# Attention phase: three PSUM banks for the row maxima and one for the scores, in place of two and two

## The chip, the cores and the metric

One core of a Trainium2 chip runs the kernel. The metric is the device time of one execution in microseconds (us); the time before is the median of three runs.

## The reference, cut to what matters

`x` is 8 batches of 512 rows of 512 numbers, `ctx` the same size. Two layers follow each other; each adds a gated attention and a gated feed-forward to `x`. Only the first attention is touched by the change:

```
xn = layernorm(x)                       # over the last axis
q, k, v = xn @ W_Q + b_Q, ctx @ W_K + b_K, ctx @ W_V + b_V   # 16 heads of 32
scores = einsum('bhqd,bhkd->bhqk', q, k) / sqrt(32)
attn = softmax(scores, axis=-1)
out = einsum('bhqk,bhkd->bhqd', attn, v) # 512 numbers a row again
x = x + tanh(g_xattn[0]) * (out @ W_O + b_O)
x = x + tanh(g_ffn[0])   * ffn(layernorm(x))         # quantised weights and activations
x = x + tanh(g_xattn[1]) * attention(layernorm(x), ctx)
x = x + tanh(g_ffn[1])   * linear(mxfp4(layernorm(x)))
```

Everything is float32.

## The kernel before, in words

The program has four phases one after the other: `attention_phase` (the projections and the first attention up to the normalised heads), `prepare_weights`, `ffn_phase` and `final_phase`. A barrier and a clearing of the semaphores stand between the first and the rest. The change lies in `attention_phase` alone.

**Work of the attention phase.** The 8 batches each have G = 4 groups of J = 4 heads. A group has 16 steps i (4 heads times T = 4 tiles of 128 rows). For each step there is a *maxima* matmul (L406): queries as the weights, keys as the moving operand, 96 rows deep, because each float32 operand is kept as a high and a low part and three products are stacked. VectorE takes the negated maximum of each of its 128 rows (L565). When a group's 16 are done, `mt` (L412) transposes them, ScalarE copies them to a row (L501), and a DMA puts that row as row 97 under the stacked queries (L334). Then the *score* matmul (L423) computes the transposed scores with the maximum already subtracted, and ScalarE takes the exponential straight from PSUM into `probs` (L510). GpSimd adds up the probabilities of the four key tiles (L619, 12 adds a group). After 16 steps TensorE multiplies probabilities and values (`pv`, L434, 32 matmuls) and sums the rows (`den`, L444, 8 matmuls); VectorE takes reciprocals in four pieces (L571) and multiplies (L576), ScalarE adds a bias (L515).

**What lies between.** In the same stream TensorE makes the projections of later groups: queries and keys (L381, three matmuls a step, copied out by ScalarE as the high part, L480, and by VectorE as the low part, L557, then stored to HBM at L320 and loaded back stacked at L328), the values (L395, copied by ScalarE, L496), and the transposes of `x` and `ctx` (L365, high part by ScalarE, L471, low part by VectorE, L549). LayerNorm of `x` is done by VectorE (L536, L541), GpSimd and ScalarE (L488).

**The order** is written out by hand. `Clock` holds every step with a time; a group has a PERIOD of 160 units, of which the first 128 are 16 slots of 8 units, and the rest is for `pv` and `den`. Each engine emits its own instructions sorted by that time plus an offset of its own, for all batches, with no loop. So the order in each queue is fixed, and only semaphores decide when things start. In a slot TensorE has a maxima matmul of a later group (19 slots ahead of its scores), a score matmul, and what projection work falls there. ScalarE's copies L480 and L471 stand between the exponentials; `mt`'s copy L501 stands before the exponential of slot 14.

**PSUM** has eight banks of 128 x 512 float32: two `work` banks for projections and transposes (given out by `Turns`), two `mx` for the maxima, two `sc` for the scores, one `pvb`, one `den`. A wait before a matmul says that its bank has been read. For the maxima it is `mx_done` (one count per reduce, L565), for the scores `exp_done` (one per exponential, L510); both are for the count that leaves one later instruction open, since there are two banks:

```
wait_count(pe, mx_done, it, shift, G * T * J, g * T * J + i - 1)
wait_count(pe, exp_done, it, shift, G * T * J, g * T * J + i - 1)
```

The third number of `wait_count` is the count per batch, the last the count within it; it emits a wait on the product of both, and none if that isn't positive.

Of the kernel before, what the change touches and what calls it, by code (L numbers as in the profile page):

```python
# [5 lines left out]
ALU = mybir.AluOpType  # L6
ACT = mybir.ActivationFunctionType
AX = mybir.AxisListType

P = 128  # L10
# [124 lines left out]
def attention_phase(nc, NB, x, ctx_in, w_q, b_q, w_k, b_k, w_v, b_v, spill, attn_t, ctx_t):  # L135
# [4 lines left out]
    T, C, G, J = S // P, D // P, D // P, P // DH  # L140
# [6 lines left out]
    with ExitStack() as ctx:  # L147
# [3 lines left out]
        def pb(name):  # L151
            return ctx.enter_context(nc.psum_tensor("a_" + name, [P, 512], F32))
# [28 lines left out]
        eps = sb("eps", [P, 1], F32)  # L181

        work = [pb("work0"), pb("work1")]
        mx = [pb("mx0"), pb("mx1")]
        sc = [pb("sc0"), pb("sc1")]
        pvb, den = pb("pvb"), pb("den")

        w_loaded, w_hi, w_lo = [sem(f"w_loaded_{n}") for n in "qkv"], sem("w_hi"), sem("w_lo")
# [86 lines left out]
        for shift, name, args in ck.order():  # L275
            if name == "t":
                users.append((shift, ("t", args[0])))
            elif name in ("qk", "v") and args[-1] == 0:
                users.append((shift, (name, *args[:-1])))
        turns = Turns(work, users, NB, read_out)  # L280

        def stage_wait(engine, it, shift, i):
            wait_count(engine, loaded[i % STAGE], it, shift, 2 * T // STAGE, i // STAGE + 1, 16)

        with nc.Block() as block:
# [60 lines left out]
            def _(pe):  # L346
# [7 lines left out]
                def window(it, shift, name, args):  # L354
                    if name == "t":
                        i, = args
                        if isinstance(it, int) and it + shift == 0 and i == T - 1:
                            turn_biases()
                        if i < T:
                            wait_count(pe, ln_done, it, shift, T, i + 1)  # L360
                        else:
                            stage_wait(pe, it, shift, i)
                        turns.wait_free(pe, it, "t", i)
                        for c in range(C):
                            last = nc.tensor.transpose(turns.bank("t", i)[:, c * P:(c + 1) * P],  # L365
                                                       stage[:, i % STAGE, c * P:(c + 1) * P], ident[:])
                        last.then_inc(t_full, 1)
                    elif name == "qk":
                        g, side, c = args
                        if c == 0:  # L370
                            if isinstance(it, int) and it + shift == 0 and g == 0:
                                pe.wait_ge(w_hi, side + 1)
                                pe.wait_ge(w_lo, side + 1)
                                pe.wait_ge(bias_done, 1)
                            n = T if side == Q else 2 * T
                            wait_count(pe, t_hi, it, shift, 2 * T, n)
                            wait_count(pe, t_lo, it, shift, 2 * T, n)
                            turns.wait_free(pe, it, "qk", g, side)
                        src = xt if side == Q else ct
                        for n, (a, m) in enumerate(PASSES):  # L380
                            last = nc.tensor.matmul(turns.bank("qk", g, side)[:], w["qk"[side]][:, c, a, g * P:(g + 1) * P],  # L381
                                                    src[:, c, m, :], start=c == 0 and n == 0, stop=c == C - 1 and n == 2)
                        if c == C - 1:
                            last.then_inc(qk_full, 1)
                    elif name == "v":
                        i, c = args
                        if c == 0:
                            if isinstance(it, int) and it + shift == 0 and i == 0:
                                pe.wait_ge(w_hi, 3)
                                pe.wait_ge(wv_lo, 1)  # L390
                            wait_count(pe, t_hi, it, shift, 2 * T, T + i + 1)
                            wait_count(pe, t_lo, it, shift, 2 * T, T + i + 1)
                            turns.wait_free(pe, it, "v", i)
                        for n, (a, m) in enumerate(PASSES):
                            last = nc.tensor.matmul(turns.bank("v", i)[:], ct[:, c, a, i * P:(i + 1) * P], w["v"][:, c, m, :],  # L395
                                                    start=c == 0 and n == 0, stop=c == C - 1 and n == 2)
                        if c == C - 1:
                            last.then_inc(v_full, 1)
                    elif name == "max":
                        g, i = args  # L400
                        j, t = i // T, i % T
                        if i == 0:
                            wait_count(pe, stacked[g][Q], it, shift, 1, 1, 48)
                            wait_count(pe, stacked[g][K], it, shift, 1, 1, 48)
                        wait_count(pe, mx_done, it, shift, G * T * J, g * T * J + i - 1)
                        nc.tensor.matmul(mx[i % 2][:], stack[0:96, g, Q, j, t * P:(t + 1) * P], stack[0:96, g, K, j, :],  # L406
                                         start=True, stop=True).then_inc(mx_full, 1)
                    elif name == "mt":
                        g, = args
                        wait_count(pe, mx_done, it, shift, G * T * J, (g + 1) * T * J)  # L410
                        wait_count(pe, recip_done, it, shift, G * T, (g - 1) * T)
                        nc.tensor.transpose(den[0:J * T, 0:P], negmax[:, g % 2].rearrange("p j t -> p (j t)"), ident[:])\  # L412
                            .then_inc(mt_full, 1)
                    elif name == "score":

                        g, i = args
                        k, j = i // J, i % J
                        if i == 0:
                            if isinstance(it, int) and it + shift == 0 and g == 0:
                                pe.wait_ge(pool_consts, 3)  # L420
                            wait_count(pe, mrow_put[g % 2], it, shift, G // 2, g // 2 + 1, 16)
                        wait_count(pe, exp_done, it, shift, G * T * J, g * T * J + i - 1)
                        nc.tensor.matmul(sc[i % 2][:], stack[0:97, g, K, j, k * P:(k + 1) * P], stack[0:97, g, Q, j, :],  # L423
                                         start=True, stop=True).then_inc(s_full, 1)
                    elif name == "pv":
                        g, k = args
                        wait_count(pe, exp_done, it, shift, G * T * J, g * T * J + (k + 1) * J)
                        if k == 0:
                            wait_count(pe, attn_done, it, shift, G, g)
                        if g == 0:  # L430
                            wait_count(pe, v_done, it, shift, T, k + 1)
                        for j in range(J):
                            h = g * J + j
                            last = nc.tensor.matmul(pvb[DH * j:DH * (j + 1), :], v[:, k, h * DH:(h + 1) * DH], probs[:, k, j, :],  # L434
                                                    start=k == 0, stop=k == T - 1)
                        last.then_inc(pv_full, 1)
                    elif name == "den":
                        g, = args
                        wait_count(pe, acc_done, it, shift, G * (T - 1) * J, (g + 1) * (T - 1) * J)
                        wait_count(pe, recip_done, it, shift, G * T, g * T)  # L440
                        last_group = isinstance(it, int) and it + shift == NB - 1 and g == G - 1
                        wait_count(pe, mt_done, it, shift, G, g + 1 if last_group else g + 2)
                        for j in range(J):
                            last = nc.tensor.matmul(den[DH * j:DH * (j + 1), :], ones[:], acc[:, j, :], start=True, stop=True)  # L444
                        last.then_inc(den_full, 1)
# [3 lines left out]
            def _(act):  # L449
# [9 lines left out]
                def window(it, shift, name, args):  # L459
# [42 lines left out]
                    elif name == "score":  # L502
# [4 lines left out]

                            wait_count(act, pv_full, it, shift, G * T, (g - 1) * T + k + 1)
                        wait_count(act, acc_done, it, shift, G * (T - 1) * J, ((g - 1) * (T - 1) + max(k, 1) - 1) * J + j + 1)
                        nc.scalar.activation(probs[:, k, j, :], sc[i % 2][:], ACT.Exp, scale=SCALE).then_inc(exp_done, 1)  # L510
                    elif name == "bias":

                        g, = args
# [6 lines left out]
            def _(dve):  # L520
# [10 lines left out]
                def window(it, shift, name, args):  # L531
# [27 lines left out]
                    elif name == "max":  # L559
# [2 lines left out]
                        wait_count(dve, mx_full, it, shift, G * T * J, g * T * J + i + 1)  # L562
                        if i == 0:
                            wait_count(dve, mt_full, it, shift, G, g - 1)
                        nc.vector.tensor_reduce(negmax[:, g % 2, j, t:t + 1], mx[i % 2][:], axis=AX.X, op=ALU.max,  # L565
                                                negate=True).then_inc(mx_done, 1)
                    elif name == "recip":
                        g, q = args
# [1024 lines left out]
```

## Time and profile before

| | us |
|---|---|
| median of 3 runs | 1709.39 |
| lowest and highest | 1706.91, 1711.35 |
| the profiled execution | 1708.97 |
| its span | 1707.2 |
| TensorE busy | 1513.5 (89%) |
| VectorE busy | 1233.4 (72%) |
| GpSimd busy | 905.9 (53%) |
| ScalarE busy | 873.6 (51%) |

The span is that of the profile, from the first to the last instruction; what lies around it belongs to the execution's time. A row of the timeline gives the start from the span's beginning, the duration, the engine, the line of the kernel, the operation, output and inputs by name with their shape, and how many instructions of the kind follow each other (x3); where the engine was idle before, a bracket says for how long and which instruction released it ("issue" is a release that the profile ties to no instruction). PE is TensorE's matmul, PEld its weight load, which runs beside the matmul ahead of it; DVE is VectorE, ACT ScalarE, POOL GpSimd. Names that begin with a_ belong to the attention phase: a_mx are the maxima's banks, a_sc those of the scores, a_negmax the maxima, a_part the projection before it is stored, a_stack the stacked operands.

### The profile page before, as it was taken

To read this page: it belongs to the slowest core of one execution; us is meant where nothing else is said; L and a number is where in the kernel's file an instruction comes from. 1 tells how busy PE (TensorE), PEld (TensorE's weight loads), DVE (VectorE), ACT (ScalarE), POOL (GpSimd) and SP (SyncE) were. 2 spreads that over 40 slices of the span, in tenths; PEclk is the share of its full clock that TensorE was granted. 3 is DMA by queue.
4 is the path that set the end of the run, shared out by engine and by line. 5 is a ranking of instruction groups with operands and counts; after the bars stand their busy time and mean duration, and the time that the engine had idled before them with its cause. 6 is when DMAs were issued, how large, how long until landed. Compare 5 with 4: busy or idle time off the path is not lost. (4 is left out here: it accounts for less than half of the span.)

```text
span 1707.2 us, 25251 instructions
## 1 busy us (share of the span) xinstructions
PE 1513.5 (89%) x7272; PEld 981.8 (58%) x7305; DVE 1233.4 (72%) x2149; ACT 873.6 (51%) x1433; POOL 905.9 (53%) x1162
## 2 busy tenths in 40 slices
PE   4799999998999999998446899999999939999997
PEld 3556666665656666663135455555555417888885
DVE  3567776777767776666374688888888717999985
ACT  3255555555555555554365545555555415555552
POOL 3168566676658566666301433443444115777774
PEclk9899999999999999997667999999999969999998
DMA  5827456473827456470271444444444353445420
GB/s 187 256 63 207 145 159 194 130 216 111 244 79 204 146 157 198 118 204 13 98 272 37 78 107 113 111 110 106 113 111 110 66 185 118 137 148 182 139 68 37
DMA packets 198430, 233.90 MB, mean 137 GB/s; under 512 B 97196, under 2 KB 114104, under 8 KB 194744
## 3 DMA queue, kind: packets, MB, share of 16 engines
q1 hardware_dynamic: 198328, 232.68, 47.3%
q8 instruction: 47, 0.77, 0.2%
q14 instruction: 55, 0.45, 0.1%
HBM read 135.86 MB, written 75.53 MB: 124 GB/s over the span
## 5 line engine op out<-in xcount | busy, mean ns | idle before, releaser
L510 ACT ACTIVATE a_probs<-a_sc 128x512 f32<-128x512 f32 x512 | 300.3, 596 | 298.7 <-PE a_sc L423 296.2
L565 DVE TENSOR_REDUCE a_negmax<-a_mx 128x1 f32<-128x512 f32 x512 | 338.0, 675 | 99.2 <-PE a_mx L406 98.3
L619 POOL TENSOR_TENSOR a_acc<-a_acc,a_probs 128x512 f32<-128x512 f32 x256 | 320.9, 1283 | 6.0 <-ACT a_probs L510 4.4
L619 POOL TENSOR_TENSOR a_acc<-a_probs 128x512 f32<-128x512 f32 x128 | 161.7, 1284 | 243.5 <-ACT a_probs L510 242.6
L406 PE MATMUL a_mx<-a_stack 96*128 96x512 f32 x512 | 227.0, 443 | 32.9 <-DVE a_negmax L565 20.8
L1002 PE MATMUL bank<-w_wgu,b_xq 128*128 128x512 bf16 x1022 | 227.7, 381 | 7.6 <-DMA b_xq<-b_xcode 7.6
L423 PE MATMUL a_sc<-a_stack 97*128 97x512 f32 x512 | 216.2, 424 | 9.5 <-DMA a_stack<-a_mrow 7.5
L571 DVE RECIPROCAL a_attn<-a_den 128x128 f32<-128x128 f32 x128 | 120.8, 948 | 121.5 <-PE a_den L444 121.5
L1002 PEld LDWEIGHTS bank<-w_wgu,b_xq 128*128 128x128 bf16 x1024 | 100.4, 98 | 130.0 <-DMA b_xq<-b_xcode 8.5
L406 PEld LDWEIGHTS a_mx<-a_stack 96*128 96x128 f32 x512 | 100.8, 197 | 102.1 <-DVE a_negmax L565 51.1
L1041 ACT ACTIVATE b_sig<-bank,b_tok 128x512 f32<-128x512 f32 x128 | 87.6, 684 | 92.4 <-PE bank L1002 89.2
L381 PE MATMUL a_work<-a_xt,a_w_q 128*128 128x512 f32 x384 | 119.7, 426 | 13.0 <-DVE a_xt L549 13.0
L423 PEld LDWEIGHTS a_sc<-a_stack 97*128 97x128 f32 x512 | 102.9, 201 | 35.9 <-ACT a_probs L510 10.5
L1009 PE MATMUL bank<-w_wd,b_hq 128*128 128x512 bf16 x481 | 113.0, 387 | 11.2 <-DMA b_hq<-b_hcode 9.1
L434 PE MATMUL a_pvb<-a_probs,a_v 128*32 128x512 f32 x1024 | 121.2, 615 | 0.0
L1096 DVE TENSOR_TENSOR b_hid<-b_sig,bank 128x512 f32<-128x512 f32 x128 | 87.5, 685 | 46.2 <-ACT b_sig L1041 46.1
L1045 ACT ACTIVATE b_hid<-b_hid,b_htok 128x2048 f32<-128x2048 f32 x32 | 64.1, 2002 | 104.7 <-DVE b_htok L1115 104.7
L381 PE MATMUL a_work<-a_ct,a_w_k 128*128 128x512 f32 x384 | 111.9, 402 | 1.5 <-DVE a_ct L549 1.5
L395 PE MATMUL a_work<-a_w_v,a_ct 128*128 128x512 f32 x384 | 112.1, 404 | 0.0
L991 PE MATMUL bank<-w_wo,b_apart 128*128 128x512 f32 x384 | 102.7, 417 | 8.1 <-POOL b_apart L1148 7.2
L1154 POOL TENSOR_TENSOR b_nmean<-b_mv,w_minus 128x1 f32<-128x1 f32 x32 | 6.1, 191 | 178.9 <-DVE b_mv L1068 178.9
L1347 PE MATMUL bank<-c_ct,c_xt 128*128 128x512 f32 x384 | 96.2, 400 | 5.3 <-DVE c_xt L1428 5.3
(177 smaller groups left out, 2733.2 us busy)
## 6 DMA issues: line engine op xcount, KB each, us to landing
a_stack<-spill SPq DMA_DIRECT2D x192, 256.0 KB, 4.9
spill<-a_part SPq DMA_DIRECT2D x64, 512.0 KB, 3.4
ctx_t<-a_ct SPq DMA_DIRECT2D x16, 1024.0 KB, 8.5
c_ct<-ctx_t SPq DMA_DIRECT2D x8, 2048.0 KB, 8.1
a_stage<-in_x_dram SPq DMA_DIRECT2D x32, 256.0 KB, 5.0
a_stage<-in_ctx_dram SPq DMA_DIRECT2D x32, 256.0 KB, 2.7
attn_t<-a_attn SPq DMA_DIRECT2D x32, 256.0 KB, 3.0
b_xin<-in_x_dram SPq DMA_DIRECT2D x32, 256.0 KB, 2.7
```

The lines of the kernel that those rows point to most:

```text
L381: last = nc.tensor.matmul(turns.bank("qk", g, side)[:], w["qk"[side]][:, c, a, g * P:(g + 1) * P], src[:, c, m, :], start=c == 0 and n == ...
L395: last = nc.tensor.matmul(turns.bank("v", i)[:], ct[:, c, a, i * P:(i + 1) * P], w["v"][:, c, m, :], start=c == 0 and n == 0, stop=c == C ...
L406: nc.tensor.matmul(mx[i % 2][:], stack[0:96, g, Q, j, t * P:(t + 1) * P], stack[0:96, g, K, j, :], start=True, stop=True).then_inc(mx_full, 1)
L423: nc.tensor.matmul(sc[i % 2][:], stack[0:97, g, K, j, k * P:(k + 1) * P], stack[0:97, g, Q, j, :], start=True, stop=True).then_inc(s_full, 1)
L434: last = nc.tensor.matmul(pvb[DH * j:DH * (j + 1), :], v[:, k, h * DH:(h + 1) * DH], probs[:, k, j, :], start=k == 0, stop=k == T - 1)
L510: nc.scalar.activation(probs[:, k, j, :], sc[i % 2][:], ACT.Exp, scale=SCALE).then_inc(exp_done, 1)
L565: nc.vector.tensor_reduce(negmax[:, g % 2, j, t:t + 1], mx[i % 2][:], axis=AX.X, op=ALU.max, negate=True).then_inc(mx_done, 1)
L571: nc.vector.reciprocal(attn[:, g % 2, q * P:(q + 1) * P], den[:, q * P:(q + 1) * P]).then_inc(recip_done, 1)
L619: nc.gpsimd.tensor_tensor(acc[:, j], probs[:, 0, j] if k == 1 else acc[:, j], probs[:, k, j], ALU.add)\
L991: last = nc.tensor.matmul(bank_o[:], apart[:, t % 2, a, c, :], wo[:, c, m, :], start=c == 0 and n == 0, stop=c == C - 1 and n == 2)
L1002: last = nc.tensor.matmul(bank[:], xq[:, t % 2, c, :], wgu[:, side, c, m * 512:(m + 1) * 512], start=c == 0, stop=c == C - 1)
L1009: last = nc.tensor.matmul(bank_d[:], hq[:, t % 2, r, :], wd[:, r, :], start=r == 0, stop=r == R - 1)
```

## The change

PSUM bank `sc1` becomes `mx2`. The maxima rotate through three banks, counted on through all groups and batches (16 steps a group isn't a multiple of 3), and their matmul waits for one reduce less. All scores go to one bank, and their matmul waits for the exponential just before it. No instruction is added, taken out or moved in any queue.

```diff
-        mx = [pb("mx0"), pb("mx1")]
-        sc = [pb("sc0"), pb("sc1")]
+        mx = [pb("mx0"), pb("mx1"), pb("mx2")]
+        sc = pb("sc0")
...
+        def max_bank(b, g, i):
+
+            return ((b * G + g) * T * J + i) % 3
...
-                        wait_count(pe, mx_done, it, shift, G * T * J, g * T * J + i - 1)
-                        nc.tensor.matmul(mx[i % 2][:], stack[0:96, g, Q, j, t * P:(t + 1) * P], stack[0:96, g, K, j, :],
+                        wait_count(pe, mx_done, it, shift, G * T * J, g * T * J + i - 2)
+                        nc.tensor.matmul(mx[max_bank(it + shift, g, i)][:], stack[0:96, g, Q, j, t * P:(t + 1) * P], stack[0:96, g, K, j, :],
...
-                        wait_count(pe, exp_done, it, shift, G * T * J, g * T * J + i - 1)
-                        nc.tensor.matmul(sc[i % 2][:], stack[0:97, g, K, j, k * P:(k + 1) * P], stack[0:97, g, Q, j, :],
+                        wait_count(pe, exp_done, it, shift, G * T * J, g * T * J + i)
+                        nc.tensor.matmul(sc[:], stack[0:97, g, K, j, k * P:(k + 1) * P], stack[0:97, g, Q, j, :],
...
-                        nc.scalar.activation(probs[:, k, j, :], sc[i % 2][:], ACT.Exp, scale=SCALE).then_inc(exp_done, 1)
+                        nc.scalar.activation(probs[:, k, j, :], sc[:], ACT.Exp, scale=SCALE).then_inc(exp_done, 1)
...
-                        nc.vector.tensor_reduce(negmax[:, g % 2, j, t:t + 1], mx[i % 2][:], axis=AX.X, op=ALU.max,
+                        nc.vector.tensor_reduce(negmax[:, g % 2, j, t:t + 1], mx[max_bank(it + shift, g, i)][:], axis=AX.X, op=ALU.max,
```

## Rows read from the trace of the kernel before

**Rows 1.** Stretches: bounds, length, each engine's busy us, granted clock, DMA; mean of six of 100 us.
```profile
386.50:393.70 7.20, 4.28 (x24) 2.71 (x22) 7.20 (x13) 4.84 (x10) 1.85 (x2) 1.00 0.51 146
...
sum 600.00, PE 569.73 PEld 372.44 DVE 436.42 ACT 329.50 POOL 399.41; mean PE 94.96 PEld 62.07 DVE 72.74 ACT 54.92 POOL 66.57
```
**Rows 2.** Waits from 0 to 830 us: who for whom, total us, times, longest.
```profile
PEld a_mx L406 <- DVE a_negmax L565: 51.1, 78, 1.7
...
PE a_work L381 <- DVE a_xt L549: 13.0, 8, 1.6
...
PEld a_sc L423 <- ACT a_probs L510: 10.5, 26, 0.9
```
**Rows 3.** Timeline, slots of projections (412) and of values (465): start, us, instruction.
```profile
411.83 0.40 PE L423 MATMUL a_sc<-a_stack 97*128 97x512 f32 x1
...
412.07 0.85 PE L381 MATMUL a_work<-a_ct,a_w_k 128*128 128x512 f32 x3
412.27 0.60 ACT L510 ACTIVATE a_probs<-a_sc 128x512 f32<-128x512 f32 x1 [0.56 <-PE a_sc L423]
...
412.99 0.40 PE L423 MATMUL a_sc<-a_stack 97*128 97x512 f32 x1
...
415.77 0.69 ACT L480 ACTIVATE a_part<-a_work,a_bias 128x512 fp32r<-128x512 f32 x1
...
464.88 0.40 PE L423 MATMUL a_sc<-a_stack 97*128 97x512 f32 x1
...
466.06 0.40 PE L423 MATMUL a_sc<-a_stack 97*128 97x512 f32 x1
```
**Rows 4.** Timeline, a score matmul that an exponential held up.
```profile
421.76 1.78 ACT L510 ACTIVATE a_probs<-a_sc 128x512 f32<-128x512 f32 x3
...
422.40 0.19 PEld L423 LDWEIGHTS a_sc<-a_stack 97*128 97x128 f32 x1 [0.23 <-ACT a_probs L510]
...
422.45 0.45 PE L423 MATMUL a_sc<-a_stack 97*128 97x512 f32 x1
```
**Rows 5.** Timeline, slot 14 of a group.
```profile
403.95 0.39 PE L423 MATMUL a_sc<-a_stack 97*128 97x512 f32 x1
...
404.49 0.27 ACT L501 ACTIVATE a_mrow<-a_den 16x128 fp32r<-16x128 f32 x1
404.67 0.57 ACT L510 ACTIVATE a_probs<-a_sc 128x512 f32<-128x512 f32 x1
```
**Rows 6.** Timeline, scores of group 1 and its first projection; first score a batch later.
```profile
386.18 0.40 PE L423 MATMUL a_sc<-a_stack 97*128 97x512 f32 x1
...
386.65 0.40 PE L423 MATMUL a_sc<-a_stack 97*128 97x512 f32 x1
...
387.56 0.40 PE L423 MATMUL a_sc<-a_stack 97*128 97x512 f32 x1
...
393.69 1.47 PE L381 MATMUL a_work<-a_xt,a_w_q 128*128 128x512 f32 x3 [1.64 <-DVE a_xt L549]
...
396.24 0.63 PE L423 MATMUL a_sc<-a_stack 97*128 97x512 f32 x1
...
482.28 0.40 PE L423 MATMUL a_sc<-a_stack 97*128 97x512 f32 x1
```
**Rows 7.** Timeline, two weight loads of the maxima that waited.
```profile
425.87 0.19 PEld L406 LDWEIGHTS a_mx<-a_stack 96*128 96x128 f32 x1 [1.55 <-issue]
...
439.86 0.19 PEld L406 LDWEIGHTS a_mx<-a_stack 96*128 96x128 f32 x1 [0.81 <-DVE a_negmax L565]
```
**Rows 8.** Timeline, the last group: first scores, first adds, a held score, row sums.
```profile
812.41 0.73 PE L423 MATMUL a_sc<-a_stack 97*128 97x512 f32 x2
...
815.98 4.97 POOL L619 TENSOR_TENSOR a_acc<-a_probs 128x512 f32<-128x512 f32 x4 [4.69 <-ACT a_probs L510]
...
822.68 0.79 PE L423 MATMUL a_sc<-a_stack 97*128 97x512 f32 x1 [0.20 <-ACT a_probs L510]
...
830.81 1.06 PE L444 MATMUL a_den<-a_acc,a_ones 128*32 128x512 f32 x8 [1.83 <-POOL a_acc L619]
```

## The prediction

> **What bounds the kernel now.** I read the stretches of the span first, then the waits of the attention phase, then the timeline of one batch slot by slot. In the steady stretch TensorE is busy 95% of the time and no other engine is above 73% [rows 1]. Only the attention phase (to about 840 us) uses the edited banks; what follows it starts when it ends, so every microsecond gained or lost there goes to the end. The unit of the work is the slot: one maxima matmul, one score matmul, and what the order puts between (three projection matmuls, four transposes, or nothing). A slot with three projection matmuls takes 1.16 us (score at 411.83, next at 412.99), one with three of the values' 1.18 (464.88 to 466.06) [rows 3], one with nothing else 0.47 (386.18 to 386.65), one with four transposes 0.91 (386.65 to 387.56) [rows 6]. The waits show what the two-bank rings cost today: the maxima's weight loads stand 51.1 us for VectorE's reduces in the whole phase, the scores' 10.5 us for the exponentials [rows 2].
>
> **The scores: one bank.** Score i may now start only when exp i-1 is through, and everything queued behind it on TensorE waits too. The price is the loop score, exp, next score. A score matmul of the trace that was held by an exp shows it whole: the exp ends at 421.76+0.60 = 422.36, the weight load starts at 422.40 (0.04), the matmul ends at 422.45+0.45 = 422.90, so 0.50 after the load began [rows 4]; an exp starts 0.04 after its matmul ends (411.83+0.40, then 412.27) and takes 0.60 [rows 3]. Sum 0.04+0.50+0.04+0.60 = 1.18 us. No slot can be shorter. The bounds: 1.08 if only the matmul's own 0.40 counted, and 1.30 if the loop also has to pass a ScalarE copy; I take 1.18, the row that is this very wait. So the 1.16 and 1.18 slots cost 0.02 and nothing, a transpose slot 0.27, an empty slot 0.71.
> Two slots are worse. Where a projection ends, its copy by ScalarE (0.69, L480) can start only at 0.24+0.85+0.04 = 1.13 after the score [rows 3], and lets the next exp in at about 1.73 (the second start lies 0.1 before the first's end, as 0.27 of copy and 0.18 to the next start show at 404.49 [rows 5]) where it was due at 0.44+1.18 = 1.62: 0.11 more, with the load about 0.12, slot 1.30. And in slot 14 the small copy L501 stands ahead of that slot's exp: score 403.95, exp 404.67 to 405.24 [rows 5], then 0.04, and 0.11 for a load that could not be made ahead (0.50 less the matmul's own 0.40): slot 1.44.
>
> **The maxima: three banks.** Maxima matmul i waits for reduce i-3 instead of reduce i-2. This removes waits such as the 0.81 us at 439.86 [rows 7], but not those where VectorE is itself behind: from 386.5 to 393.7 VectorE is busy 7.20 of 7.20 us (reciprocals, reduces, low parts of the transposes) [rows 1], and TensorE's next projection waits for its last transpose part until 393.69 [rows 6]. Its instructions don't change, so that stretch keeps its 7.5 us from 386.18. That also hides the score loop there: five slots of 1.18 make 5.9.
>
> **One batch, group by group** (groups 1, 2, 3 and 0 of the next; the slots before are the 64 differences between the starts of its scores, from 386.18 to 482.28 [rows 6]).
> Group 1: nothing before 393.69; then, at half clock (0.63 for a matmul), the score at 396.24 [rows 6] waits for an exp that ends near 396.66 and its load: +0.57; a transpose slot with a projection copy 0.91 to 1.30: +0.39; an empty slot +0.71; two projection slots +0.04; slot 14 from 1.19 to 1.44: +0.25; two transpose slots already held to 1.13 and 1.23 by reduces: 0. GpSimd's adds, which held the row sums there by 0.30, are in time now: -0.30. Sum +1.66.
> Group 2: +0.77 to score 415.81, nearly all the empty slot at 412.99. From there a chain of copy, store and refill decides: the first maxima matmul of the next group waits for its operand to land, its load idle 1.55 us until 425.87 [rows 7]. The slots between would grow by some 0.5 but end inside that wait: 0. After it slot 14 from 1.27 to 1.44 and small change: +0.20. Sum +0.97.
> Group 3: the empty slot and two LayerNorm copies of ScalarE put the fourth score 0.78 late; the two waits for reduces after it go (slots of 1.81 and 1.41 become 1.18): -0.86; an empty slot already held to 0.96: +0.22; two projection copies +0.23; slot 14 +0.17; rest +0.04. Sum +0.58.
> Group 0: fourteen slots with the values' matmuls, 1.18 against 1.18: about 0.1 in all. Slot 14 has nothing else in it, 0.60 to 1.44: +0.84. Sum +0.95.
> Between groups TensorE has 5.5 us of probability and row-sum matmuls without a score; they cover the last exp, and the refill of the row of maxima gets later cover, not earlier. SP's and GpSimd's queues lose nothing: no instruction is moved.
> Seven batches of 1.66+0.97+0.58 = 3.21 give 22.5 us; eight groups 0 give 7.6.
>
> **The last batch's groups 1 to 3** have no projections left, so almost every slot is short, and what ends them is GpSimd: twelve adds of 4.97/4 = 1.24 us after the fifth exp; the last row sums waited for them [rows 8]. In group 3 the scores start at 812.41 and the first add at 815.98. With the loop the fifth exp is through at 812.41+4x1.18+1.04 = 818.17, 2.2 later; that is the lower bound. But the scores there run at half clock (0.79 us for a held one [rows 8]), where the loop is 0.05+0.79+0.04+0.60 = 1.48, longer than an add: 812.41+4.72+11x1.48+1.04+1.28 = 835.7 against 830.8, so +4.9. TensorE is as idle there in either kernel, so I take the half clock, and 4 us for each of the three groups: 12.
> Sum 22.5+7.6+12 = 42.1. The profiled execution took 1708.97 us, span and 1.8 around it, within its sisters' spread (median 1709.39). Forecast 1751.
>
> The trace fits what the Trainium skill states against this edit: "Perfetto Trace Analysis", Optimizing Tensor Performance, has independent matmul groups rotate through banks so that one is read out while the next is computed. By that rule alone a single bank would add read-out to every matmul, an exp and its start, 0.64, for each of 512 scores (8 batches, 4 groups, 16 slots), some 328 us as an estimate from the skill's rule and this trace's exp; the rows show why it is far less, since 0.70 us of other matmuls lie in most slots.
>
> **Rivals.**
> A. The weight load doesn't wait with its matmul: it is done ahead, and the loop is 0.04+0.40+0.04+0.60 = 1.08. Against it: the held load at 422.40 begins after the exp, not before [rows 4]. Per batch an empty slot then costs 0.60, a transpose slot 0.17, copies nothing: about 2 us a batch, 16 in all, and 9 for the last batch: 1734. The Trainium skill has this as a rule, "TensorE: Matmul & The Clock Gate" (Architectural detail: the queue pulls weight loads ahead of matmuls in flight); the row shows it for loads without a wait only.
> B. The stalls bring TensorE down to half clock more often. In group 1 this happens after the 386 to 393 stretch: three projection matmuls take 1.47 at 393.69 and 0.85 at 412.07 [rows 3, 6], 0.2 us each, some eight of them, 1.6 a spell. One more spell a batch, of which group 1's second half with its short slots is the candidate, adds 8x1.6 = 13: 1764. For it: the last batch does fall at such a load; against: slots of 1.18 with five matmuls leave it nearly full.
> C. The other side: the new stalls only take the place of old ones. The loop's gross cost, if nothing hid it, is eight empty slots 5.7, six transpose slots 1.6, slots 14 2.1 and the rest 1.1 a batch, 74 us in seven, and 12 at the end: 86. The old waits are 51.1 (maxima) and 13.0 (projections for the transposes) [rows 2], 8 for the refills of group 2 (seven of 1.15), and 11 for the half-clock spells: 83. If all went, the time would be 1712. It decides if nearly all of these waits vanish, the stretch before 393.69 above all: with less than 81 us given back the kernel is slower by more than can be overlooked. Some 3 us of each batch's waits are VectorE's own load, which speaks against it. For truly faster, a loop under 1.1 would have to come on top.
>
> **Numbers.** My forecast 0.47, A 0.16, B 0.27, C 0.10. Under 0.3% (5 us) a measurement of this kernel doesn't tell from none. Faster 0.04 and same 0.08 are C and the far end of A; slower 0.88. The range 1722 to 1778 goes from between C and A to B with a loop of 1.2 to 1.3 in the other slots (0.1 in some 25 slots a batch is 18 us, part of it hidden).
>
> **What would show it.** Right: scores never closer than 1.18 us; their weight loads idle behind exps tens of us (now 10.5) and the maxima's behind reduces far less than 51.1; group 0 longer by 1, group 1 by 1.7, a batch 100.3 us instead of 96.1 (386.18 to 482.28); the last row sums near 873 instead of 830.8. Wrong: scores 1.08 apart after a held load (A), more half-clock spells (B), the 386 to 393 stretch shorter than 7.5 (C), or exps starting later than 0.04 after their scores in many slots, which would mean ScalarE's copies cost more than 0.12.

## The result, and the profile after

| | before | after |
|---|---|---|
| median | 1710.4 us (4 runs) | 1750.9 us (4 runs) |
| lowest and highest | 1706.9, 1711.4 | 1750.1, 1756.2 |
| ratio, 95% interval | | 1.0247 [1.0222, 1.0273] |
| span of the profiled execution | 1707.2 | 1748.6 |

The kernel became 40.5 us slower by the medians (their ratio is 1.0237; the one in the table comes from all runs and lies a little higher). 1751 had been forecast, so the sum was right. Two of its terms were not: group 1 cost 8.9 us less than forecast and the last batch 10.6 us more. They made up for each other, with a part that lay outside all terms.

Stretches of the changed kernel: the one in which VectorE is the bound, and the mean of six of 100 us from 150 on (columns as in [rows 1]).
```profile
398.80:406.00 7.20, 5.12 (x23) 2.85 (x21) 7.20 (x13) 5.28 (x10) 1.55 (x2) 1.00 0.45 121
...
sum 600.00, PE 559.37 PEld 336.15 DVE 423.94 ACT 327.94 POOL 382.93; mean PE 93.23 PEld 56.03 DVE 70.66 ACT 54.66 POOL 63.82
```
TensorE, busy 95% before, is down to 93%, and VectorE from 73% to 71%: the stage runs slower, and no engine has taken TensorE's place. VectorE is again busy 7.20 of 7.20 us at the start of group 1.

Of the waits of the attention phase, the one that answers to the last of [rows 2] (who for whom, total us, times, longest):
```profile
PEld a_sc L427 <- ACT a_probs L514: 190.4, 456, 1.5
```
The scores' weight loads now stand 190.4 us for the exponentials in 456 of 512 cases, where it was 10.5 in 26 [rows 2]. The maxima's waits for the reduces, 51.1 there, are gone. What ended the idle time of the maxima's matmuls and loads together (us, times), in the kernel before and then in the changed one:
```profile
  DVE a_negmax L565: 72.0, 115
```
```profile
  DVE a_negmax L569: 1.6, 2
```

Timeline of the changed kernel, the stretch that answers to [rows 6], and in it two held scores, then a score that didn't wait and one held behind it:
```profile
398.52 0.40 PE L427 MATMUL a_sc<-a_stack 97*128 97x512 f32 x1
...
399.68 0.50 PE L427 MATMUL a_sc<-a_stack 97*128 97x512 f32 x1 [0.52 <-ACT a_probs L514]
...
400.21 0.60 ACT L514 ACTIVATE a_probs<-a_sc 128x512 f32<-128x512 f32 x1 [0.59 <-PE a_sc L427]
...
400.87 0.50 PE L427 MATMUL a_sc<-a_stack 97*128 97x512 f32 x1
...
406.03 0.94 PE L385 MATMUL a_work<-a_xt,a_w_q 128*128 128x512 f32 x3 [1.12 <-DVE a_xt L553]
...
407.05 0.39 PE L427 MATMUL a_sc<-a_stack 97*128 97x512 f32 x1
...
408.13 0.19 PEld L427 LDWEIGHTS a_sc<-a_stack 97*128 97x128 f32 x1 [0.89 <-ACT a_probs L514]
408.13 0.50 PE L427 MATMUL a_sc<-a_stack 97*128 97x512 f32 x1 [0.46 <-ACT a_probs L514]
```
The loop is there: a score matmul from 399.68 to 400.18, its exp from 400.21 to 400.81, the next score at 400.87, 1.19 us after the first. The slots of 0.47 and 0.91 have gone from the steady stretch; 1.18 to 1.20 is the commonest length. The stretch from the group's first score to the projection that waits for VectorE takes 406.03-398.52 = 7.51 us, and took 393.69-386.18 = 7.51 [rows 6]: in it the new waits cost nothing. The idle time before that projection has gone from 1.64 to 1.12 us, and the projection takes 0.94 us for its three matmuls instead of 1.47: no half clock follows. From this first score of group 1 to the next batch's it is 98.8 us, where 100.3 had been forecast and 96.1 was measured before.

**Where the 41.4 us of span went.** The start of the row sums (L444, after: L448) marks the end of each group. Between the first of the 32 marks and the 29th lie seven groups of each kind:

| | forecast | profiles, after less before |
|---|---|---|
| to the first mark (98.03, 99.75) | 0.9 | 1.7 |
| seven groups 1 | 11.6 | 2.7 |
| seven groups 2 | 6.8 | 7.8 |
| seven groups 3 | 4.1 | 4.6 |
| seven groups 0 | 6.7 | 6.3 |
| last three groups | 12 | 22.6 |
| from the last mark to the end | 0 | -4.2 |
| sum | 42.1 | 41.4 |

The last line but one of the table is unchanged code. From the last mark to the end of the span the ten kernels below and the changed one take 870.3 to 873.8 us; the 876.4 of the profile before is the odd one. It is of the size of the spread of the runs and is taken here for the chance of one execution; that isn't shown.

The last batch of the changed kernel, end of group 1 (before, the last of its kind is in [rows 8]):
```profile
811.21 0.79 PE L427 MATMUL a_sc<-a_stack 97*128 97x512 f32 x1 [0.26 <-ACT a_probs L514]
...
812.69 0.79 PE L427 MATMUL a_sc<-a_stack 97*128 97x512 f32 x1 [0.26 <-ACT a_probs L514]
...
815.25 5.78 PE L438 MATMUL a_pvb<-a_probs,a_v 128*32 128x512 f32 x32
...
816.03 1.27 POOL L623 TENSOR_TENSOR a_acc<-a_acc,a_probs 128x512 f32<-128x512 f32 x1 [0.21 <-ACT a_probs L514]
820.86 1.03 PE L448 MATMUL a_den<-a_acc,a_ones 128*32 128x512 f32 x8
```
The same 32 matmuls in the last group of the kernel before:
```profile
823.41 5.58 PE L434 MATMUL a_pvb<-a_probs,a_v 128*32 128x512 f32 x32
```
At half clock each slot takes 1.48 us, as worked out (thirty slots of this length in the whole trace). But GpSimd's last add ends at 817.30, and the row sums start at 820.86: what ends the group is the run of 32 matmuls at half clock behind the last score. The run was nearly as long before (5.58 us), but there it was through at 828.99, and the row sums waited 1.83 us more for GpSimd [rows 8]. The forecast had GpSimd end the group in the changed kernel too. Of the three groups the row sums start 3.6, 2.7 and 2.6 us behind GpSimd's last add, where before it was at most 0.2.

### The profile page after: what moved, and what is told of

It reads as the page before. It is cut to its first block and busy times, and to the rows that moved or that the text cites. A ratio compares the mean times of both kernels' runs of the same rounds, so it can differ in the third digit from the quotient of the medians.

```text
span 1748.6 us, 25280 instructions
## 1 busy us (share of the span) xinstructions
PE 1528.8 (87%) x7272; PEld 951.3 (54%) x7305; DVE 1233.4 (71%) x2149; ACT 883.0 (50%) x1433; POOL 904.8 (52%) x1162
## 5 line engine op out<-in xcount | busy, mean ns | idle before, releaser
L514 ACT ACTIVATE a_probs<-a_sc 128x512 f32<-128x512 f32 x512 | 304.2, 594 | 329.7 <-PE a_sc L427 324.3
L427 PE MATMUL a_sc<-a_stack 97*128 97x512 f32 x512 | 240.3, 469 | 68.6 <-ACT a_probs L514 59.0
L410 PE MATMUL a_mx<-a_stack 96*128 96x512 f32 x512 | 215.4, 421 | 7.0 <-DMA a_stack<-spill 5.3
L427 PEld LDWEIGHTS a_sc<-a_stack 97*128 97x128 f32 x512 | 99.3, 194 | 202.3 <-ACT a_probs L514 190.4
L1013 PE MATMUL bank<-w_wd,b_hq 128*128 128x512 bf16 x481 | 112.4, 386 | 10.7 <-DMA b_hq<-b_hcode 8.6
L385 PE MATMUL a_work<-a_xt,a_w_q 128*128 128x512 f32 x384 | 113.6, 408 | 9.2 <-DVE a_xt L553 9.2
```

Source lines behind the costliest of these rows:

```text
L410: nc.tensor.matmul(mx[max_bank(it + shift, g, i)][:], stack[0:96, g, Q, j, t * P:(t + 1) * P], stack[0:96, g, K, j, :], start=True, stop=T ...
L427: nc.tensor.matmul(sc[:], stack[0:97, g, K, j, k * P:(k + 1) * P], stack[0:97, g, Q, j, :], start=True, stop=True).then_inc(s_full, 1)
L514: nc.scalar.activation(probs[:, k, j, :], sc[:], ACT.Exp, scale=SCALE).then_inc(exp_done, 1)
L1013: last = nc.tensor.matmul(bank_d[:], hq[:, t % 2, r, :], wd[:, r, :], start=r == 0, stop=r == R - 1)
```

## The experiments

Medians are given with the ratio to the kernel before of the same chip and hour, and its 95% interval.

**One score bank, two for the maxima.** The change's loss alone.
```diff
-        mx = [pb("mx0"), pb("mx1"), pb("mx2")]
+        mx = [pb("mx0"), pb("mx1")]
...
-            return ((b * G + g) * T * J + i) % 3
+            return i % 2
...
-                        wait_count(pe, mx_done, ..., g * T * J + i - 2)
+                        wait_count(pe, mx_done, ..., g * T * J + i - 1)
```


> One bank for the scores, two for the maxima: the loss of the change without its gain. If the score loop (1.18 us) makes the loss and the third maxima bank gives part of it back, the maxima's waits return in the slots where VectorE is late (some 0.9 us a batch in group 3, 0.9 in groups 1 and 2), and perhaps the half-clock spells at the start of each group 1 (1.6 us each): 1757 to 1775 us. Rival: at the slower pace of 1.18 us a slot the reduces keep up with two banks, and the third is worth nothing: within 2 us of the changed kernel's 1751.

Measured: 1756.6 us, 1.0282 [1.0260, 1.0304]; the interval overlaps that of the change, and the median lies between the two expectations, just under the first. What ended the idle time of the maxima here:
```profile
  DVE a_negmax L569: 20.0, 52
```
That is 20.0 us of waits instead of 1.6, and 72.0 in the kernel before: the pace of one score bank alone takes most of them away. But where there is no half clock the groups have the same lengths: 24.1 us for group 3 and 24.6 for group 0 with either number of banks, 25.5 for group 1. The 8.3 us between the two profiles' marks 1 and 29 are 8.0 in groups 1, and three of these are long ones (29.3, 27.0, 28.2) with half clock in them. So the rival is right on what the waits are worth: at the pace that one score bank sets, the third maxima bank gives nothing directly. Whether it keeps the clock up stays open: other kernels with three banks had such spells as well.

**The row of maxima's copy later.**
```diff
-                  act_qk=6, dve_qk=11, act_v=8, dve_max=5, act_exp=5, mt=-46, mrow=8, act_mt=3, acc=12,
+                  act_qk=6, dve_qk=11, act_v=8, dve_max=5, act_exp=5, mt=-46, mrow=8, act_mt=4, acc=12,
```


> The changed kernel with ScalarE's copy of the row of maxima one unit later in its order, so that it stands behind the exponential of slot 14 and not ahead of it. If slot 14 really is 1.44 us because of that copy, each of 31 groups is 0.26 us shorter: about 8 us, 1743. Rival: the slot is held by something else (the transpose of the maxima on TensorE), or the group then waits for the row's DMA: no change, 1751.

Measured: 1754.1 us, 1.0266 [1.0240, 1.0292], no gain. Yet the term is real: slot 14 falls from 1.44 to 1.18 us in group 1 and from 1.35 to 1.09 in group 0, and the groups without half clock are shorter by 0.26 (1), 0.19 (3) and 0.28 (0) us. Three groups 1 with half clock (26.7, 27.9, 29.1 for 25.2) take 8 us in this profile and give it all back. Neither theory had that.

**Two score banks in the last batch.**
```diff
+        def score_bank(b, g, i):
+            return work[0] if b == NB - 1 and g > 0 and i % 2 else sc
...
-                        wait_count(pe, exp_done, it, shift, G * T * J, g * T * J + i)
+                        wait_count(pe, exp_done, it, shift, G * T * J, g * T * J + i - (it + shift == NB - 1 and g * T * J + i > T * J))
...
```


> The changed kernel, but in groups 1 to 3 of the last batch the scores alternate between their bank and the first work bank, which nothing uses any more there. If the last batch's 22.6 us are the loop at half clock (1.48 us a slot), they go: about 1728 us, and the loss that is left is that of the seven batches before. Rival: the last batch is slow because of the clock or GpSimd's adds alone, with two banks as with one: more than 1745.

Measured: 1729.5 us, 1.0121 [1.0094, 1.0148]: 21.4 less than the changed kernel, as the theory has it. The last three groups take 59.2 us, with one bank 84.2, before 61.6.

**Filler matmuls in the last batch.**
```diff
+                        if it + shift == NB - 1 and g > 0:
+                            for c in range(3):
+                                nc.tensor.matmul(work[0][:], w["q"][:, c, HI, 0:P], xt[:, c, HI, :], start=True, stop=True)
```


> The changed kernel with three added matmuls behind each score in groups 1 to 3 of the last batch, whose results nobody reads. If half clock is what makes the loop 1.48 instead of 1.18 there, TensorE stays at full clock and 48 slots are up to 0.3 us shorter although 144 matmuls are added: the last group is then held by GpSimd's adds, so 12 to 14 us less, about 1738. Rival: the loop doesn't depend on the clock in this way, and the added work costs its time: 1751 or more.

Measured: 1737.9 us, 1.0174 [1.0153, 1.0195]: 13.0 less, with 144 matmuls more. Group 2 of the last batch, first in the changed kernel, then with the filler (stretches as in [rows 1]; the last but two column is the granted clock):
```profile
822.20:848.90 26.70, 20.61 (x62) 7.50 (x64) 12.27 (x18) 10.30 (x18) 15.22 (x12) 0.62 0.03 11
```
```profile
815.50:840.00 24.50, 23.67 (x125) 14.49 (x121) 12.43 (x18) 10.31 (x18) 15.02 (x12) 1.00 0.03 12
```
The last three groups take 72.5 us with the filler, 84.2 without and 61.6 in the kernel before. So at full clock 12 of the last batch's 22.6 us go, and 11 stay for the loop and whatever the filler itself costs. The kernel before has half clock there too, with its slots mostly shorter.

**The third bank alone.** Eight banks have no room for three and two beside the others, so the row sums are written over the products of probabilities and values. The products are lost by that, so these two kernels leave out the result of the attention and serve for the time alone; the instructions and their order stay. The first kernel has only that (with a wait more before the first product and another before the maxima's transpose), the second the third bank too.
```diff
-        pvb, den = pb("pvb"), pb("den")
+        pvb = pb("pvb")
+        den = pvb
...
+                            wait_count(pe, mt_done, it, shift, G, g + 1 if last_group else g + 2)
...
-                        wait_count(pe, recip_done, it, shift, G * T, (g - 1) * T)
+                        wait_count(pe, attn_done, it, shift, G, g - 1)
```


> The kernel before with the row sums written into the bank of the probability-value products (one bank less), so that the division of products by sums is left out in effect: the instructions and their order are the same. Expected: the time of the kernel before within 3 us, 1707 to 1713. It is the base for the next kernel.

> As the kernel just before it (row sums written over the products), with the freed bank as a third for the maxima, and still two for the scores: the gain of the change without its loss. Theory: the third bank removes the maxima's waits where VectorE catches up within a slot or two (some 2 us a batch, mostly in group 3 and at the end of group 1), not the stretch at the start of group 1 in which VectorE is busy without a pause: 12 to 18 us less, or 25 if the half-clock spell after that stretch goes too. Rival: it removes nearly all of the 51 us of waits: 1660 or less. Second rival: the waits only move to the next instruction that needs VectorE, and nothing is gained: within 4 us of the base.

Measured: 1710.1 us, 0.9994 [0.9975, 1.0012], and 1706.1 us, 0.9976 [0.9959, 0.9992]. The third bank is worth some 4 us, which isn't clear of noise, since the intervals of the two overlap; 12 to 18 us had been expected, and the second rival (within 4 us of the base) comes closest. The waits of the maxima with two banks and then with three:
```profile
  DVE a_negmax L568: 70.9, 114
```
```profile
  DVE a_negmax L571: 18.3, 33
```
What became of the 53 us between them is seen group by group. Group 3 is 22.60 instead of 23.44 us: 0.84 less, the forecast's 0.86. Group 1 without a long spell is 24.5 for 24.9. But group 0 is 24.7 where it was 23.9. Its first score, with three banks:
```profile
453.02 0.27 ACT L507 ACTIVATE a_mrow<-a_pvb 16x128 fp32r<-16x128 f32 x1 [0.68 <-PE a_pvb L416]
...
457.88 0.52 SPq L338 DMA_DIRECT2D a_stack<-a_mrow  x1
...
462.24 0.19 PEld L427 LDWEIGHTS a_sc<-a_stack 97*128 97x128 f32 x1 [2.27 <-DMA a_stack<-a_mrow]
```
TensorE arrives there earlier and waits 2.27 us for the row of maxima: copied by 453.29, its DMA was issued at 457.88, behind three loads of the stack that SP's queue issued from 456.49. In the whole profile the scores stood 24.1 us for this DMA with three banks and 10.7 with two. So part of the gain turned into a DMA wait one group later.

**Filler matmuls at the start of group 1,** on the kernel before (six a batch) and on the changed one (five).
```diff
                             n = T if side == Q else 2 * T
+                            turns.wait_free(pe, it, "qk", g, side)
+                            if g == 0 and side == Q and it + shift > 0:
+                                for f in range(6):
+                                    nc.tensor.matmul(turns.bank("qk", g, side)[:], w["q"][:, f % C, HI, 0:P], w["k"][:, f % C, HI, :],
+                                                     start=True, stop=True)
                             wait_count(pe, t_hi, it, shift, 2 * T, n)
                             wait_count(pe, t_lo, it, shift, 2 * T, n)
-                            turns.wait_free(pe, it, "qk", g, side)
```


> The kernel before with six added matmuls a batch on constant operands, whose results nobody reads, placed where TensorE stands waiting for VectorE's last low part at the start of group 1 (1.64 us of idle matmul time there). Theory: the half-clock spell of every group 1 comes from the little that TensorE does in that stretch; with it filled the clock stays full and the spell's 1.5 us goes in seven batches: 1698 to 1701 us against 1709, group 1 at 23.4 us instead of 24.9. Rival: the spell has another cause, or the added matmuls push the projection back: 1708 or more.

> The changed kernel with five such filler matmuls a batch in the same place. In it the spells come in some batches only (none in its profile, two to four in those of its variants), so their absence should take 0 to 3 us from the median and narrow its spread: 1747 to 1750, group 1 at 25.5 us in every batch. Rival: spells go on coming in some batches: 1751 to 1756.

Measured: on the kernel before 1704.2 us, 0.9960 [0.9946, 0.9973]; on the changed one 1751.8, 1.0235 [1.0205, 1.0265]. The filler, and the projection behind it, in the kernel before (compare 393.69 in [rows 6]):
```profile
391.55 1.53 PE L379 MATMUL a_work<-a_w_k,a_w_q 128*128 128x512 f32 x6
393.35 0.93 PE L385 MATMUL a_work<-a_xt,a_w_q 128*128 128x512 f32 x3 [0.27 <-DVE a_xt L553]
...
407.98 1.07 PE L448 MATMUL a_den<-a_acc,a_ones 128*32 128x512 f32 x8 [0.31 <-POOL a_acc L623]
```
Three matmuls in 0.93 us instead of 1.47. Group 1 is 23.85 us in six of seven batches instead of 24.88; in the seventh the spell still came. That is less than the 1.5 expected. The first eight slots of the group do fall by that, from 11.70 to 10.16 us, but now GpSimd's adds hold the row sums, which start 4.72 us after the last score instead of 4.23. And in the profile seven groups 0 are 2.2 us longer: again part of it waits elsewhere. In the changed kernel all seven groups 1 are without half clock (25.4 to 25.5), but so they were in its own profile; the median doesn't move. It lies in the rival's range, though the spells that the rival counted on aren't in the profile; all that can be said is that there was nothing left to win here.

**The filler, and three banks for the last batch's maxima,** on the kernel before: the first work bank joins them from step 3 of group 2, when nothing else uses it.
```diff
+        def max_bank(b, g, i):
+            n = g * T * J + i - 2 * T * J - 3
+            return [work[0], mx[1], mx[0]][n % 3] if b == NB - 1 and n >= 0 else mx[i % 2]
...
-                        wait_count(pe, mx_done, it, shift, G * T * J, g * T * J + i - 1)
+                        wait_count(pe, mx_done, it, shift, G * T * J, g * T * J + i - 1 - (it + shift == NB - 1 and g * T * J + i >= 2 * T * J + 3))
...
```


> As the kernel with the filler, and in the last batch the maxima of groups 2 and 3 also use the first work bank, free by then: three banks for them without taking one from the scores. Theory: the reduces' waits of the last batch go (the two profiles with the row sums merged show 61.7 us for the last three groups with two banks, 59.5 with three): 2 us less than the kernel with the filler alone, about 1697. Rival: GpSimd's adds end those groups with either number of banks: no difference.

Measured: 1701.0 us, 0.9939 [0.9916, 0.9962]. Its last three groups take 59.3 us against 62.0 with the filler alone. It is the fastest of all, 0.6% under the kernel before and some 3% under the changed one; its interval overlaps that of the filler alone, so the last step shows in the groups and not clearly in the time. In its profile three of seven groups 1 have a spell in spite of the filler (24.9 us), so the filler makes the spells rarer and doesn't end them.

**All of it on the changed kernel** (filler, later copy, two score banks in the last batch).

> The changed kernel with all that the runs so far point to: filler in group 1, the row of maxima's copy behind the exponential of slot 14, and two score banks in the last batch. From the profiles' groups without spells, 25.2+24.45+23.9+24.3 = 97.85 a batch, 685 in seven, and 59.2 for the last three groups: about 1719 us, which is what the one score bank costs in the steady stretch alone, still slower than before by some 10. Rival: the losses were only hidden by each other, and it is below 1712.

Measured: 1721.0 us, 1.0058 [1.0037, 1.0079]. No half clock in any steady group; the groups are 25.2, 24.7, 23.9 and 24.35 us. Between marks 1 and 29 it takes 687.1 us, where the kernel before with its filler takes 667.1: some 20 us are what one score bank costs in seven batches, after what these edits gave back. The expectation of 1719 holds, and the rival (below 1712) doesn't.

## Why the prediction was right

**The loop: right.** 1.18 us was forecast from one held matmul, and 1.19 measured. One thing was worded wrongly: starts of scores are as little as 1.08 us apart, which was to have spoken for rival A. The recorded start of a held matmul is 0.1 us early, since it comes with its load. A score at 407.05 ends at 407.44, the next, held, is recorded from 408.13 to 408.63, its start together with that of its load: from end to end 1.19. In a held score the load begins after the exp, in 456 cases; A falls.

**Slot 14 and the projection's copy: right in kind.** Slot 14 is 1.44 in group 1, as forecast, 1.35 to 1.37 in the others; the later copy took 0.26 off it in groups 1 and 0 and 0.07 in the other two. Slots after a projection are 1.26 or 1.27, not 1.30.

**The covered parts: right.** The stretch bound by VectorE kept its 7.51 us, group 3 rose by 4.6 us for 4.1, group 2 by 7.8 for 6.8, group 0 by 6.3 for 6.7 in seven batches.

**Group 1: wrong by 9 us.** The step that failed is "at half clock (0.63 for a matmul), the score at 396.24": the half clock was taken over from the trace of before, and the changed kernel has none there. Between 386.5 and 393.7 TensorE was busy 4.28 us before [rows 1] and 5.12 in the changed kernel, and the idle time ahead of the projection fell by half a microsecond; the granted clock of the six stretches of 100 us, 0.97 or 0.98 before, is 1.00 in all. The first eight slots of the group took 11.70 us before, 10.16 with the filler on that kernel, so without a spell, and 10.88 in the changed kernel. So the spell had cost 1.5 us and the loop adds 0.7 to these slots: 0.8 us less, where 0.57 more was forecast. A second, smaller step was wrong as well: GpSimd's adds didn't hold the row sums by 0.30 (the matmul at 409.37 follows the one before without idle time), so nothing came back there. In the profile before, one group 1 (26.3) had a longer spell, which is another 1.4 of the 9.

Rival B (more spells) failed in its place, the steady groups of this profile. Three variants of the changed kernel had three groups with a spell each and one had one, of 1.5 to 3.9 us, which is as much as the terms of the sum, and after first slots of the same lengths. What decides whether a spell comes isn't shown; with one profile for each kernel, neither is whether it differs by the kernel or by the execution.

**The last batch: wrong by 11 us.** The loop at half clock was right to the hundredth. The step that failed is "what ends them is GpSimd": with the slots at 1.48 the 32 product matmuls, 5.78 us at half clock, come after the last score, and the row sums start 3.6, 2.7 and 2.6 us behind the last add in the three groups, 8.9 in all. Taking 4 us for each group where the working gave 4.9 left out another 2.7. Two score banks there bring the whole back.

**Rival C: wrong.** The waits for reduces did go, nearly all of the 51.1 us, and gave back no more than the forecast had for group 3. The experiments show why: with one score bank the slower pace takes most of them away by itself, and with two, part of what the third bank takes away comes back as a wait for a DMA. The Trainium skill's rule to rotate matmul groups through banks ("Perfetto Trace Analysis", Optimizing Tensor Performance) gave the sign; its size came from the slots.

That 1751 was met to the microsecond is luck: -8.9, +10.6 and the -4.2 at the end are each larger than the difference that is left. What stays open is whether the 4.2 us at the end have a cause beyond the execution; a single profile of before was taken for it.

## What to carry to other kernels

A ring of one costs the whole loop of producer and reader, and only the slots shorter than that loop pay: lay the loop, measured on one held instruction, against each slot length, and look for what would have waited anyway. A ring's waits are no measure of what another bank brings: waits of 71 us fell to 18, and the time by some 4. When a stage slows down, work out anew what ends it, with every duration at the clock that the trace shows there. A price measured at half clock holds only as long as the half clock itself stays.

## What was not expected of the hardware

In the kernel before, idle times of TensorE of 1.3 and 1.6 us preceded a spell of half clock in every batch. The same stretch of the changed kernel and its variants, with the idle time spread among the scores, had a spell in some batches or none; one spell makes its group 1.0 to 3.9 us longer. Matmuls whose results nobody reads paid for themselves twice: six a batch in a wait took 7 us off the kernel before, and 144 in the last batch 13 us off the changed one, where the granted clock rose from 0.62 to 1.00.
